# High and low halves for all six pieces of the experts' down projection

## The chip, the cores and the metric

The kernel runs on one core of a Trainium2 chip. The metric is the device time of one execution in microseconds. Lower is better. A core has five engines that run their own instruction streams and meet only at semaphores: PE (matmuls), DVE, ACT, POOL and SP, which here only issues the DMAs.

## The reference

A network of nine blocks on 256 tokens of 192 channels: four attention blocks and five mixture-of-experts blocks, each behind a layer norm and added to its input. The expert blocks that matter here (0, 1 and 3; 3 stands in the reference's "conv" place) compute, with W1 of 192x768 and W2 of 768x192 for each expert:

```
t = layer_norm(x)
gates = softmax or top-2 of (t @ Wg)          # 8 experts, some with a ninth that all tokens use
h = act(t @ W1[e] + b1[e])                    # relu, tanh-gelu, gelu
y = h @ W2[e] + b2[e]
x = x + sum over e of gates[:, e] * y
```

Every expert is computed for all tokens and its result is weighted by the gate. Block 2 gathers tokens instead, and block 4 has a gated form with a hidden size of 384.

## The kernel before

All of it is one program for one core, with the order of each engine written out by hand and a counting semaphore for each kind of result. Tokens are two tiles of 128. Blocks 0, 1 and 3 have 8, 8 and 9 experts, 25 in all. Experts 0 and 1 are written out, the middle ones run in a loop of two per turn, and the last ones are written out again.

The weights are float32. To use the faster fp32r matmul without losing precision the up projection is made from halves: `w1_hi` is a rounded copy made by ACT, `w1_lo` is the difference made by DVE (line 1193, three instructions of 128x512 per expert, called w_lo in the trace), and x has halves as well. The up projection of one expert is 30 matmuls of 256 columns (line 951) in three parts b = 0, 1, 2. After each part ACT makes two pieces of hid (line 600).

The down projection has six pieces of 128 hidden channels. Before, the first two (part b = 0) are plain float32 matmuls of 192 columns (line 963, each of which the trace shows as two records), and the last four use halves: DVE casts hid to `hid_hi` (line 1267) and subtracts to `hid_lo` (line 1269), POOL makes the high half of the down weights by a multiplication by one (line 443) and the low half by a subtraction (line 445). For each piece and token tile PE then does hid_hi times both halves of W2 (384 columns, line 975) and hid_lo times the high half (192 columns, line 977). The products with W2's low half are kept in their own 192 columns and DVE adds both column groups to x (lines 1282 and 1288, "the adds").

What sets the order around this:

- PE: up projection of expert g, then its down projection, then expert g+1. The down projection waits for the adds of the expert before, since both use the same two banks.
- ACT: hid of the three parts, then the three copies to `w1_hi` for the next expert. After expert 0 of a block it also makes the exponentials of the router's logits (`logit_exps`, line 582), from which DVE makes the gates (lines 1243 to 1250) before the first adds.
- DVE: halves of hid for two parts, three `w1_lo` of the next expert, the adds.
- POOL: halves of W2 of the next expert, each as soon as PE has released the part of `w2_hl` (`w2_used`, and `y_psum` for the last).
- The layer norm ahead of a block: DVE's statistics, the power on POOL (line 391), four DVE instructions that make xn (lines 1047 and 1050), PE's transposes (line 653), xT on ACT and DVE, the first up part, and the router's matmuls (line 928). POOL's program puts the split of expert 0's W2 right after the power. PE does some matmuls on a constant (line 661) while it waits.

## Time and profile before

| | us |
|---|---|
| median of 3 runs | 514.72 (511.82 to 517.03) |
| the profiled execution | 511.37 |
| its span, first to last instruction | 509.5 |
| PE busy in it | 463.6 |
| DVE busy | 354.0 |
| ACT busy | 234.8 |
| POOL busy | 171.3 |
| mean granted clock of PE | 0.98 |

The profile is that of one execution. The span is cut by blocks roughly as follows: block 0 from 57 to 127, block 1 from 174 to 244, block 3 from 371 to 447, block 4 from 450 to the end, with attention and block 2 between them. Busy is the time in which an engine executes an instruction, and that includes time in which an instruction that has started cannot go on. An idle time in brackets stands ahead of an instruction, with what ended it.

### The profile page before, as it was taken

The page shows a single profiled execution, that of the slowest core. Times are in us where ns is not written, and L with a number is a line of the kernel's source. Part 1 is how long each engine was busy: PE and PEld are TensorE (multiplying, and loading weights), DVE is VectorE, ACT ScalarE, POOL GpSimd, SP SyncE. Part 2 cuts the span into 40 slices and gives each one's busy share as a digit, 9 for nine tenths or more (in the row PEclk, how much of TensorE's full clock was granted, in tenths as well). Part 3 has the DMA queues.
Part 4 walks back from the last instruction along what each step waited for, and adds up shares of the span by engine and source line. Part 5 has one row for each costly group of instructions (what it writes and reads, how often), then busy time and mean ns, then how long its engine had stood idle before and what let it go on. Part 6 is the DMA issues. An engine that isn't in the chain of part 4 may idle for free.

```text
span 509.5 us, 8914 instructions
## 1 busy us (share of the span) xinstructions
PE 463.6 (91%) x3064; PEld 382.4 (75%) x3064; DVE 354.0 (69%) x780; ACT 234.8 (46%) x594; POOL 171.3 (34%) x171
## 2 busy tenths in 40 slices
PE   4989699999889799999889988899969999989997
PEld 3755499999555499999645654555759999979997
DVE  6575588998476578998476467451179899868764
ACT  1267245544156366555156337423218555627443
POOL 6026324673025415754006214310033665500000
PEclk8999999999999989999999999999989999989999
DMA  5380025650191015551169500602313555525551
GB/s 146 121 248 1 1 96 183 184 187 1 65 305 40 0 64 196 180 175 39 43 170 322 176 0 1 186 2 93 124 37 134 185 185 176 191 58 166 200 177 36
DMA packets 19347, 62.36 MB, mean 122 GB/s; under 512 B 4025, under 2 KB 6898, under 8 KB 19314
## 3 DMA queue, kind: packets, MB, share of 16 engines
q1 hardware_dynamic: 19314, 61.93, 38.0%
q8 instruction: 20, 0.33, 0.3%
q14 instruction: 13, 0.11, 0.1%
HBM read 59.82 MB, written 2.10 MB: 122 GB/s over the span
## 4 chain that ended last, share of the span: by engine, by line
PE 69%; DVE 11%; issue 10%; POOL 4%; DMA 3%; ACT 1%; SPq 1%; POOLq 0%; DVEq 0%
PE bank L951 24%; PE bank L963 10%; PE bank L975 7%; PE bank L766 6%; PE bank L805 3%; PE bank L977 3%; PE bank L792 3%; DVE xn L1047 3%; PE bank L661 2%; POOL rstd L391 1%; DMA rel<-rel_scratch 1%; PE bank L653 1%; PE bank L773 1%; DVE nmax L1153 1%; PE bank L674 1%
## 5 line engine op out<-in xcount | busy, mean ns | idle before, releaser
L951 PE MATMUL bank<-xT_hi,w_hi 128*128 128x256 f32 x408 | 111.7, 295 | 0.0
L600 ACT ACTIVATE hid<-bank,b 128x256 f32<-128x256 f32 x150 | 62.7, 471 | 71.0 <-PE bank L951 70.8
L1193 DVE TENSOR_TENSOR w_lo<-w,w_hi 128x512 fp32r<-128x512 f32 x102 | 93.0, 950 | 2.2 <-ACT w_hi L552 0.3
L951 PE MATMUL bank<-xT_hi,w_lo 128*128 128x256 f32 x408 | 82.6, 284 | 0.0
L443 POOL TENSOR_TENSOR w_hl<-w,consts 128x384 fp32r<-128x384 f32 x50 | 52.4, 1048 | 85.1 <-PE bank L977 85.1
L951 PEld LDWEIGHTS bank<-xT_hi,w_hi 128*128 128x128 f32 x408 | 79.2, 194 | 1.5 <-issue 1.1
L423 POOL TENSOR_TENSOR probs<-probs,rinv 128x512 f32<-128x512 f32 (+1 forms) x44 | 42.8, 991 | 101.0 <-DVE rinv L1157 100.9
L951 PEld LDWEIGHTS bank<-xT_hi,w_lo 128*128 128x128 f32 x408 | 64.3, 194 | 0.0
L975 PE MATMUL bank<-w_hl,hid_hi 128*128 128x384 f32 x200 | 61.7, 373 | 0.0
L445 POOL TENSOR_TENSOR w_hl<-w,w_hl 128x384 fp32r<-128x384 f32 x50 | 57.9, 1158 | 3.9
L963 PE MATMUL bank<-w,hid 128*128 128x192 f32 x308 | 56.5, 327 | 2.3 <-issue 2.3
L951 PE MATMUL bank<-xT_lo,w_hi 128*128 128x256 f32 x204 | 58.3, 286 | 0.0
L552 ACT ACTIVATE w_hi<-w 128x512 fp32r<-128x512 f32 x102 | 58.3, 626 | 0.1
L963 PEld LDWEIGHTS bank<-w,hid 128*128 128x128 f32 x308 | 49.5, 190 | 3.5 <-issue 2.9
L977 PE MATMUL bank<-w_hl,hid_lo 128*128 128x192 f32 x200 | 50.1, 251 | 0.0
L526 ACT ACTIVATE probs<-bank,nmax 128x256 f32<-128x256 f32 (+1 forms) x96 | 42.9, 461 | 10.3 <-DVE nmax L1153 10.3
L661 PE MATMUL bank<-warm 128*128 128x256 f32 x168 | 46.5, 419 | 1.2 <-DVE warm L1329 1.2
L766 PE MATMUL bank<-kT,qT 128*128 128x512 f32 (+1 forms) x96 | 42.6, 578 | 1.0 <-POOL probs L423 0.8
L951 PEld LDWEIGHTS bank<-xT_lo,w_hi 128*128 128x128 f32 x204 | 39.8, 195 | 0.2
L661 PEld LDWEIGHTS bank<-warm 128*128 128x128 f32 x168 | 33.7, 211 | 7.0 <-issue 1.9
L977 PEld LDWEIGHTS bank<-w_hl,hid_lo 128*128 128x128 f32 x200 | 38.1, 191 | 0.0
L975 PEld LDWEIGHTS bank<-w_hl,hid_hi 128*128 128x128 f32 x200 | 37.5, 188 | 0.7
(159 smaller groups left out, 674.3 us busy)
## 6 DMA issues: line engine op xcount, KB each, us to landing
w<-in_M_w_dram SPq DMA_DIRECT2D x34, 768.0 KB, 5.5
w<-in_M_w_dram SPq DMA_DIRECT2D x33, 576.0 KB, 3.9
w<-in_M_w_dram SPq DMA_DIRECT2D x9, 288.0 KB, 2.9
wqkv<-in_A_wqkv_dram SPq DMA_DIRECT2D x4, 432.0 KB, 7.0
rel_scratch<-relall SPq DMA_DIRECT2D x4, 372.0 KB, 2.3
wproj<-in_A_wproj_dram SPq DMA_DIRECT2D x4, 288.0 KB, 7.9
wqkv<-in_M_w_dram SPq DMA_DIRECT2D x2, 576.0 KB, 17.4
kT<-in_M_w_dram SPq DMA_DIRECT2D x2, 576.0 KB, 6.6
```

The lines of the kernel that those rows point to most:

```text
L443: pool.tensor_tensor(parts[:, :, 0], w, one, ALU.mult).then_inc(w2_hi_ready, 1)
L445: pool.tensor_tensor(parts[:, :, 1], w, parts[:, :, 0].bitcast(F32), ALU.subtract).then_inc(w2_lo_ready, 1)
L526: act.activation(probs[:, p % 2, t, h, 0:keys_of(n, t)], scores_bank(n, p, t)[:, h], ACT.Exp, bias=nmax[:, p % 2, t, h:h + 1], accum_out=r ...
L552: act.activation(w1_cols(w1_hi, b), w1_cols(w1[s], b), ACT.Copy).then_inc(w1_hi_ready, 1)
L600: ins = act.activation(hid[:, 2 * b + c, :], bank[B_H[b]][:, c * T:(c + 1) * T], FUNC[cfg["act"]], bias=b1[:, kb, bass.ds(at, 1)])
L661: pe.matmul(bank[b][:, 0:T], warm[:, 0:P], warm[:, :], start=True, stop=True)
L766: pe.matmul(scores_bank(n, p, t), qT[:, p, t * P:(t + 1) * P], kT[:, p, :, 0:keys_of(n, t)], start=True, stop=True).then_inc(s_psum, 1)
L951: ins = pe.matmul(bank[B_H[b]][:, c2 * T:(c2 + 1) * T], w, xs, start=(q == 0), stop=(q == 4))
L963: ins = pe.matmul(bank[B_Y[t]][:, 0:C], hid[:, c, t * P:(t + 1) * P], w2[s][:, c * C:(c + 1) * C], start=(c == 0), stop=(c == nc2 - 1), sk ...
L975: pe.matmul(out[:, 0:2 * C], hid_hi[:, c, tok], w2_hl[:, c].rearrange("p a n -> p (a n)"), start=False, stop=(c == SC - 1), skip_group_che ...
L977: ins = pe.matmul(out[:, 0:C], hid_lo[:, c, tok], w2_hl[:, c, 0], start=False, stop=(c == SC - 1), skip_group_check=True)
L1193: dve.tensor_tensor(w1_cols(w1_lo, b), w1_cols(w1[s], b), w1_cols(w1_hi, b).bitcast(F32), ALU.subtract)\
```

## The change

SB, the number of parts of the down projection with halves, becomes 3, so that no plain piece is left in blocks 0, 1 and 3.

- PE's down projection is 12 pairs of matmuls (384 and 192 columns) instead of 8 plain records and 8 pairs. Its first piece waits for `hid_lo` and `w2_lo` of part 0, where it waited for hid alone.
- `hid_hi` of part 0 is made by ACT, right after hid of part 0; DVE only subtracts for it. Parts 1 and 2 stay as they were.
- The high halves of W2 are made by ACT as copies (`split_down`), three of 128x384 per expert, behind the copies of w1, and with the same waits for PE that POOL had; POOL only subtracts, three times instead of twice. For expert 0 of a block they stand behind `x_transposed`, and for expert 1 ahead of `logit_exps`.
- `hid` has no memory of its own any more and lies in that of the attention's `probs`; a tile of block 2 moves from `hid` to `silu_g`.

```diff
-SB = 2
+SB = HB
@@
-        hid = sb("hid", [P, 2 * HB, T])
+        hid = probs[:, :, :, :, :].rearrange("p a t h k -> p (a t h) k")[:, 0:2 * HB, :]
@@
-        hplaceT = hid[:, 0:HB, :].rearrange("p c t -> p (c t)")
+        hplaceT = silu_g[:, :, :].rearrange("p c t -> p (c t)")
@@ POOL
-                pool.wait_ge(w2_in[s], 16 * (j + USED[m][s] + 1))
                 for b in range(SB):
-                    if not very_first:
-
-                        if b < SB - 1:
-                            pool.wait_ge(w2_used, g)
-                        else:
-                            pool.wait_ge(y_psum, 2 * g)
...
-                    pool.tensor_tensor(parts[:, :, 0], w, one, ALU.mult).then_inc(w2_hi_ready, 1)
                     pool.wait_ge(w2_hi_ready, SB * g + b + 1)
                     pool.tensor_tensor(parts[:, :, 1], w, parts[:, :, 0].bitcast(F32), ALU.subtract).then_inc(w2_lo_ready, 1)
@@ ACT
+            def split_down(m, j, i):
+
+                s = (i + SHIFT[m]) % 2
+                g = 2 * j + BASE[m] + i
+                very_first = isinstance(g, int) and g == 0
+                act.wait_ge(w2_in[s], 16 * (j + USED[m][s] + 1))
+                for b in range(SB):
+                    if not very_first:
+
+                        if b < SB - 1:
+                            act.wait_ge(w2_used, (SB - 1) * (g - 1) + b + 1)
+                        else:
+                            act.wait_ge(y_psum, 2 * g)
+                    at = 2 * b * C
+                    w = w2[s][:, at:at + 2 * C].rearrange("p (c n) -> p c n", c=2)
+                    act.activation(w2_hl[:, 2 * b:2 * (b + 1), 0], w, ACT.Copy).then_inc(w2_hi_ready, 1)
@@
+                        if cfg["split2"] and b == 0:
+                            act.wait_ge(h_ready, 3 * (2 * j + g) + 1)
+                            act.activation(hid_hi[:, 0:2, :], hid[:, 0:2, :], ACT.Copy).then_inc(hid_hi_act, 1)
...
                     for b in range(HB if cfg["split2"] and not last else 0):
                         split(m, j + i, 1 - i, b)
+                    if cfg["split2"] and not last:
+                        split_down(m, j + i, 1 - i)
...
+                if cfg["split2"]:
+                    split_down(m, 0, 0)
                 expert(0, 0)
                 logit_exps()
                 expert(0, 1)
@@ PE
-                                      start=False, stop=(c == SC - 1), skip_group_check=True)
+                                      start=(c == 0), stop=(c == SC - 1), skip_group_check=True)
...
-                        if c == 1:
+                        if c % 2 and c < SC - 1:
                             ins.then_inc(w2_used, 1)
@@ DVE
-                        if cfg["split2"] and b >= HB - SB:
...
+                        if cfg["split2"]:
+                            g = 2 * j + BASE[m] + i
+                            if b == 0:
+                                dve.wait_ge(hid_hi_act, g + 1)
+                            else:
+                                dve.wait_ge(h_ready, 3 * g + b + 1)
+                                dve.tensor_copy(hid_hi[:, 2 * b:2 * b + 2, :], hid[:, 2 * b:2 * b + 2, :]).then_inc(hid_hi_ready, 1)
+                                dve.wait_ge(hid_hi_ready, (SB - 1) * g + b)
+                            dve.tensor_tensor(hid_lo[:, 2 * b:2 * b + 2, :], hid[:, 2 * b:2 * b + 2, :],
+                                              hid_hi[:, 2 * b:2 * b + 2, :].bitcast(F32), ALU.subtract).then_inc(hid_lo_ready, 1)
```

## Rows read from the trace of the kernel before

**Rows 1.** The page's first part: busy us, share of the span, instructions.
```profile
PE 463.6 (91%) x3064; PEld 382.4 (75%) x3064; DVE 354.0 (69%) x780; ACT 234.8 (46%) x594; POOL 171.3 (34%) x171
```

**Rows 2.** Windows, one steady expert: start:end, us, busy us by engine, clock, DMA share, GB/s.
```profile
89.32:96.53 7.21, 7.21 (x57) 7.16 (x56) 6.84 (x12) 4.08 (x9) 4.52 (x5) 1.00 0.66 191
```

**Rows 3.** Chain that ended last, the plain down projection of a steady expert: start, us, what.
```profile
92.94 1.30 PE bank L963 x8
```

**Rows 4.** By source line, single instructions: duration ns min/median/max, first and last start.
```profile
L1193 DVE TENSOR_TENSOR w_lo<-w,w_hi x2: 1316/1410/1504, 95.6 to 96.9; 128x512 fp32r<-128x512 f32 x2
...
L445 POOL TENSOR_TENSOR w_hl<-w,w_hl x1: 1348/1348/1348, 96.5 to 96.5; 128x384 fp32r<-128x384 f32 x1
...
L445 POOL TENSOR_TENSOR w_hl<-w,w_hl x1: 1019/1019/1019, 99.1 to 99.1; 128x384 fp32r<-128x384 f32 x1
...
L1269 DVE TENSOR_TENSOR hid_lo<-hid,hid_hi x48: 691/692/694, 70.4 to 436.8; 128x512 fp32r<-128x512 f32 x48
```

**Rows 5.** Timeline of a steady expert of block 0: start, us, engine, line, instruction.
```profile
96.37 0.30 PE L951 MATMUL bank<-xT_hi,w_hi 128*128 128x256 f32 x1
...
97.90 0.84 ACT L600 ACTIVATE hid<-bank,b 128x256 f32<-128x256 f32 x2 [2.43 <-PE bank L951]
...
99.96 0.47 DVE L1267 CAST hid_hi<-hid 128x512 fp32r<-128x512 f32 x1 [0.29 <-ACT hid L600]
...
99.99 1.47 PE L963 MATMUL bank<-w,hid 128*128 128x192 f32 x8
...
100.46 0.69 DVE L1269 TENSOR_TENSOR hid_lo<-hid,hid_hi 128x512 fp32r<-128x512 f32 x1
```

**Rows 6.** Timeline of the layer norm ahead of block 0.
```profile
58.62 0.87 DVE L1047 TENSOR_SCALAR xn<-x,moments,rstd 128x192 f32<-128x192 f32 x1 [0.58 <-POOL rstd L391]
```

**Rows 7.** Timeline of the layer norm ahead of block 4.
```profile
450.85 0.38 DVE L1047 TENSOR_SCALAR xn<-x,moments,rstd 128x192 f32<-128x192 f32 x1 [0.58 <-POOL rstd L391]
```

**Rows 8.** Chain that ended last: router of block 0, gates' transposes, router of block 4.
```profile
66.50 0.64 PE bank L928 x5
...
81.91 0.22 PE bank L993 x2
...
455.90 0.64 PE bank L928 x5
```

**Rows 9.** Groups by line and shape, ACT: count | busy us, mean ns | idle before.
```profile
L552 ACT ACTIVATE w_hi<-w 128x512 fp32r<-128x512 f32 x102 | 58.3, 626 | 0.1
...
L582 ACT ACT_TABLE_LOAD x3 | 3.8, 1283 | 0.1
L564 ACT ACTIVATE hplace<-bank 128x384 f32<-128x384 f32 x8 | 3.6, 492 | 1.2 <-PE bank L859 1.2
```

**Rows 10.** Timeline of experts 0 and 1 of block 0.
```profile
69.17 0.37 DVE L1222 SCALAR_TENSOR_TENSOR sel<-consts,top_f,first 128x8 f32<-128x8 f32 x2
...
70.00 1.47 PE L963 MATMUL bank<-w,hid 128*128 128x192 f32 x8
...
73.55 0.30 PE L951 MATMUL bank<-xT_hi,w_hi 128*128 128x256 f32 x1
...
74.59 0.98 DVE L1243 TENSOR_TENSOR chosen<-expl,sel 128x16 f32<-128x16 f32 x1
...
77.24 0.73 DVE L1288 SCALAR_TENSOR_TENSOR x<-bank,gates,x 128x192 f32<-128x192 f32 x2
...
78.07 1.54 PE L963 MATMUL bank<-w,hid 128*128 128x192 f32 x8 [0.75 <-issue]
```

**Rows 11.** Timeline, PE: first transposes of the norms of block 0 and attention 1.
```profile
60.55 0.44 PE L653 MATMUL bank<-consts,xn 128*128 128x128 f32 x2 [2.36 <-DVE xn L1050]
...
129.81 0.71 PE L653 MATMUL bank<-consts,xn 128*96 128x128 f32 x4 [1.35 <-DVE xn L1047]
```

**Rows 12.** Windows with the granted clock (third figure from the end) in those two norms.
```profile
62.42:65.84 3.42, 3.42 (x12) 3.01 (x13) 2.64 (x7) 0.66 (x2) 0.00 (x0) 0.50 0.00 0
...
126.00:131.00 5.00, 3.61 (x19) 2.49 (x17) 3.54 (x13) 0.38 (x1) 0.69 (x1) 1.00 0.00 0
```

More of the change, by code:

```diff
@@ L219, in metaformer_kernel @@
         hid_hi_ready, hid_lo_ready = sem("hidden_high_ready"), sem("hidden_low_ready")
+        hid_hi_act = sem("hidden_high_first_ready")
         w2_hi_ready, w2_lo_ready, w2_used = sem("w2_high_ready"), sem("w2_low_ready"), sem("w2_parts_used")
@@ L429, in split @@
                 g = 2 * j + BASE[m] + i
-                very_first = isinstance(g, int) and g == 0
-                pool.wait_ge(w2_in[s], 16 * (j + USED[m][s] + 1))
                 for b in range(SB):
-                    if not very_first:
-                        if b < SB - 1:
-                            pool.wait_ge(w2_used, g)
-                        else:
-                            pool.wait_ge(y_psum, 2 * g)
-                    at = 2 * (HB - SB + b) * C
+                    at = 2 * b * C
                     w = w2[s][:, at:at + 2 * C].rearrange("p (c n) -> p c n", c=2)
                     parts = w2_hl[:, 2 * b:2 * (b + 1)]
-                    one = consts[:, CONST["ones"]][:, 0:1].unsqueeze(1).broadcast_to([P, 2, C])
-                    pool.tensor_tensor(parts[:, :, 0], w, one, ALU.mult).then_inc(w2_hi_ready, 1)
                     pool.wait_ge(w2_hi_ready, SB * g + b + 1)
@@ L552, in split @@
                 act.activation(w1_cols(w1_hi, b), w1_cols(w1[s], b), ACT.Copy).then_inc(w1_hi_ready, 1)
+            def split_down(m, j, i):
[9 more added lines that the diff above has]
+                            act.wait_ge(y_psum, 2 * g)
+                    at = 2 * b * C
+                    w = w2[s][:, at:at + 2 * C].rearrange("p (c n) -> p c n", c=2)
+                    act.activation(w2_hl[:, 2 * b:2 * (b + 1), 0], w, ACT.Copy).then_inc(w2_hi_ready, 1)
             def places():
@@ L1262, in hidden @@
                                 .then_inc(glu_ready, 1)
-                        if cfg["split2"] and b >= HB - SB:
-                            part = b - (HB - SB)
-                            sb2 = 2 * part
-                            dve.wait_ge(h_ready, 3 * (2 * j + BASE[m] + i) + b + 1)
-                            dve.tensor_copy(hid_hi[:, sb2:sb2 + 2, :], hid[:, 2 * b:2 * b + 2, :]).then_inc(hid_hi_ready, 1)
-                            dve.wait_ge(hid_hi_ready, SB * (2 * j + BASE[m] + i) + part + 1)
-                            dve.tensor_tensor(hid_lo[:, sb2:sb2 + 2, :], hid[:, 2 * b:2 * b + 2, :],
-                                              hid_hi[:, sb2:sb2 + 2, :].bitcast(F32), ALU.subtract).then_inc(hid_lo_ready, 1)
+                        if cfg["split2"]:
[8 more added lines that the diff above has]
+                                              hid_hi[:, 2 * b:2 * b + 2, :].bitcast(F32), ALU.subtract).then_inc(hid_lo_ready, 1)
                         if not cfg["split2"] and not last:
```

## The prediction

> **What bounds the kernel now.** I read, in this order, the page's busy times, one steady expert by windows, the chain that ended last, single experts in order of time, and the layer norms ahead of the expert blocks. PE is busy for 91% of the span [rows 1]. In the expert loops DVE is nearly full too: an expert takes 7.21 us, of which PE works 7.21, DVE 6.84, POOL 4.52 and ACT 4.08 [rows 2]. PE does 3.62 us of up projection (96.37 to 99.99) [rows 5], then 1.30 of plain down projection (8 matmul records) [rows 3], and the rest, 7.21 - 3.62 - 1.30 = 2.29, is split down projection (16 records). So PE sets the pace, and DVE has under 0.4 us to spare.
>
> DVE's 6.84 us hold a hidden part. A subtraction of 128x512 takes 0.69 us where POOL is idle (48 of hid's), but two of the three w_lo of an expert take 1.32 and 1.50 [rows 4]. These run while POOL splits the down weights, and POOL's subtraction takes 1.35 there and 1.02 alone [rows 4]. So they take turns: each waits until the other's whole instruction is done, and POOL costs DVE 0.63 + 0.81 = 1.44 us per expert.
>
> The same happens where nothing hides it. In the layer norms of blocks 0, 1 and 3 POOL splits the first expert's down weights while DVE makes xn: the first of the four xn instructions takes 0.87; in block 4, without the split, it takes 0.38 [rows 6, 7]. PE waits for them.
>
> The Trainium skill (SBUF — State Buffer, "Who interferes with whom") says that VectorE and GpSimd share a port pair that one of them holds for the whole instruction while "the other **fully blocks**". The trace agrees: 1.50 against 0.69 us.
>
> **The change, part by part.**
>
> *PE.* Per expert it takes away the 8 plain records (1.30) and adds 8 split ones. The pair of 384 and 192 columns costs 2.29/8 = 0.286, so down becomes 12 x 0.286 = 3.44 instead of 3.59: -0.15.
>
> *A new wait at the start of down.* The plain pieces needed only hid. Now the first piece needs hid's high half (ACT) and low half (DVE) of piece 0. Counted from the first up matmul, hid 0 starts on ACT at +1.53 (97.90) and takes 0.84: +2.37 [rows 5]. A wait for a result just made costs 0.04 (cast done 99.96 + 0.465, subtraction at 100.46): +2.41. The high half has the shape of an up weight's, 0.63 [rows 9]: +3.04. DVE follows with 0.04 + 0.69: +3.77. PE wakes 0.10 later (last add of expert 0 done at 77.97, first matmul 78.07) [rows 10]: +3.87. Without a stall down starts at +3.62. PE stands 0.25, plus up to 0.07 of restart (eight plain records take 1.54 there, 1.47 without a stall) [rows 5, 10]; I take 0.29. Period: 3.62 + 0.29 + 3.44 = 7.35 against 7.21, +0.14.
>
> *Does DVE follow in 7.35?* It gains a 0.61 (spacing of queued subtractions): 7.45, if POOL blocked it as before. But POOL's two high halves go to ACT, and its three subtractions start later. ACT ends the w1 copies at about +6.3; its first w2 copy, 128x384, is nearest to 0.49 (the same size from PSUM) and 0.63 (512 columns) [rows 9]; I take 0.55. POOL starts at +6.84, when two of DVE's three w_lo (from +6.0, after the later hid_lo 2) are done or running. Only the third is blocked (0.81); POOL's other two fall mostly under the adds, which take 0.73 per two beside POOL or not [rows 10]. DVE: 6.84 + 0.61 - 0.63 = 6.82, it fits. But POOL's last subtraction ends at about +3.15 of the next expert, and hid_lo 0 wants its inputs at +3.2: close (rival A). ACT, by the spacing of queued copies, about 0.1 under their length: 4.08 + 0.52 + 3 x 0.44 = 5.9 of 7.35, it fits; its third w2 copy waits for the end of down, more than 1 us before the next hid. POOL: 3 x 1.02 to 1.35, less than now.
>
> *Steady experts:* 8 + 8 + 9 less the first two of each block, 19. 19 x 0.14 = **+2.7**; bounds 19 x -0.15 = -2.9 (no stall) and 19 x 0.45 = +8.6 (DVE blocked again).
>
> *The layer norm.* POOL now has nothing to split until ACT has made a high half, which stands behind the transposed x. From the first xn to the router block 0 took 58.62 to 66.50, 7.88 us; blocks 1 and 3 show the same pattern, 7.60 and 7.87 (three such stretches, block 0's rows are shown). Block 4 needed 450.85 to 455.90, 5.05 [rows 6 to 8]. Gain 2.83 + 2.55 + 2.82 = **-8.2**. PE's granted clock was 0.50 (the 1.2 GHz level) for 3.42 us there, in block 4 too, after PE had stood 2.36 us in block 0; before attention 1 it stood 1.35 and the stretch shows 1.00 [rows 11, 12]. The idle shrinks by 1.3 to about 1.1, so the clock may stay at 2.4 GHz. It would save up to 0.09 on each of ten up matmuls, less what other engines set: -0.6 per block.
>
> *First expert's down.* Its hid_lo 0 stands on DVE behind the router's selection, done at 69.54, while down starts at 70.00 [rows 10]; 0.69 + 0.10 later is a stall of 0.35. With the higher clock PE comes earlier but DVE does not, since POOL blocks its two w_lo: 0.8. Less 0.15 for the pairs: +0.6 or +2.0 over three blocks. With the norm: -8.2 + 0.6 = -7.6, or -10.0 + 2.0 = -8.0; I take **-7.8**.
>
> *Second expert.* ACT's exponentials for the gates stood behind three w1 copies; now they stand behind the third w2 copy too, which waits for the end of down 0. They end about +1.2 into up 1, +2.5 in blocks 1 and 3 with a table load of 1.28 [rows 9]. DVE's three w_lo end at about +2.0 and its first gate instruction waits for POOL's third subtraction, to +2.9. It waited in block 0 too (0.98 us, ending 75.57, +2.02) [rows 10]. From there to the last add took 2.4. So down starts at 2.9 + 2.4 + 0.65 (hid_lo 0) + 0.1 = +6.05 where it was +4.52 (78.07 less 73.55), and then takes 3.51 where it was 3.84 (to 81.91) [rows 8]: +1.2 per block, **+3.6**; bounds 0 (if something else hides it) and +2.3 per block.
>
> Sum: 2.7 - 7.8 + 3.6 = -1.5 us. The profiled execution took 511.37 us (span 509.5) and becomes 509.9. The median of the runs is 514.72, 0.65% above that execution: 513.2.
>
> **Rivals.**
>
> *A: the turns with POOL decide (ends slower).* If POOL's last subtraction still runs when DVE wants hid_lo 0, that takes up to 0.88 more, all of it before PE's down. For: my margin is under 0.1 us. Against: a stall of PE does not delay ACT's copies, so the longer it is, the earlier POOL is done in the next expert; it damps itself. Price: period 7.66, +8.6 instead of +2.7: 519.1. It decides from a POOL end later than +3.2.
>
> *B: no stall.* If the high half and the subtraction take 0.25 less together, the period is 7.06, -2.9 instead of +2.7, and the first stall goes too (-0.9): 506.7. Against: both durations come from 48 or 102 rows that hardly vary.
>
> *C: the clock falls in a worse place.* 3.42 us at half clock cost 1.7 us of PE work. In block 4 over half of it lay on transposes and warming matmuls. If it lay on the up projection, each block gave back 1.0: 516.2. Against: less idle than before a stretch that stayed at 1.00.
>
> *D: the gate chain costs more.* Exponentials between two table loads, then hid 0 of expert 1: 1.2 more in blocks 1 and 3, 515.6. For: ACT's chain ends close behind DVE's. Against: DVE is the later of the two.
>
> **How the numbers follow.** Main forecast 0.45, 510.5 to 516 (at 513.2); A 0.18; B 0.13; C 0.12; D 0.12. 1% (5.1 us) is about what a measurement of this kernel tells from no change: under 509.6 is faster, over 519.9 slower. Faster: B's 0.13 and 0.11 of the main case, where the runs' own spread (511.82 to 517.03) or a larger clock gain carry it over. Slower: 0.10 of A, 0.06 of C and D together or with A. Same: 0.60. Range: B's 506.7 to A's 519.1, rounded outward: 506.5 to 519.5.
>
> **What would show it.** Right: xn takes 0.3 to 0.4 us in blocks 0, 1 and 3; POOL has no high halves and 75 subtractions; 300 split matmuls of each kind; steady experts of 7.3 to 7.4 us with an idle of 0.2 to 0.3 between up and down; expert 1 near 9.6 instead of 8.4; a lower mean of w_lo. Wrong: steady experts under 7.2 (B) or over 7.5 with hid_lo above 0.75 us (A); the low clock over up matmuls (C); hid 0 of expert 1 later than +4 (D). The forecast fails most easily in the steady experts, where 0.1 us each is 1.9 us.

## The result and the profile after

| | before | changed |
|---|---|---|
| median, same chip | 512.68 us | 518.42 us |
| profiled execution, span | 509.5 | 516.2 |
| PE / DVE / ACT / POOL busy | 463.6 / 354.0 / 234.8 / 171.3 | 465.9 / 357.7 / 282.7 / 156.1 |

The ratio of changed to before is 1.0084, interval [1.0052, 1.0115]: slower by 0.84%, 4.3 us. The ratio counts only executions within 1.5% of their kernel's fastest, so it is not the quotient of the two medians. The forecast of 513.2 against the median of 514.72 was a ratio of 0.997. The change was run once more on another chip, with the last experiments: 1.0051 [1.0009, 1.0093].

The page of the changed kernel, first the engines (busy us, share, instructions), then groups (count | busy us, mean ns | idle before and what ended it):

```profile
PE 465.9 (90%) x3064; PEld 381.2 (74%) x3064; DVE 357.7 (69%) x805; ACT 282.7 (55%) x694; POOL 156.1 (30%) x146
...
L436 POOL TENSOR_TENSOR w_hl<-w,w_hl 128x384 fp32r<-128x384 f32 x75 | 94.0, 1277 | 108.0 <-ACT w_hl L560 107.8
...
L990 PE MATMUL bank<-w_hl,hid_hi 128*128 128x384 f32 x300 | 94.2, 380 | 13.3 <-DVE hid_lo L1286 11.7
L1208 DVE TENSOR_TENSOR w_lo<-w,w_hi 128x512 fp32r<-128x512 f32 x102 | 90.3, 924 | 2.1
```

The parts changed as the diff says: 300 split matmuls, 75 subtractions on POOL and no multiplication there, 48 us more on ACT [rows 1]. New is the idle time of 13.3 us ahead of line 990, the first split matmul, of which 11.7 us end with `hid_lo`.

To see where the time went, I cut both executions at the same events. "Norm" runs from the first xn instruction of a block to its first up matmul, "expert 0" from there to the first up matmul of expert 1, and so on; "rest" ends with the last add of the block.

| us | before | changed | difference, three blocks |
|---|---|---|---|
| norm, blocks 0 / 1 / 3 | 5.62 / 5.63 / 5.38 | 2.88 / 2.88 / 2.88 | -7.98 |
| expert 0 | 9.31 / 9.02 / 9.54 | 9.91 / 9.84 / 9.90 | +1.78 |
| expert 1 | 8.33 / 8.33 / 8.28 | 11.05 / 11.52 / 11.51 | +9.15 |
| rest | 45.55 / 45.62 / 53.03 | 46.73 / 46.87 / 54.13 | +3.51 |
| block 4 (norm and expert 0) | 3.13 + 7.96 | 2.88 + 7.46 | -0.75 |
| all else | | | +1.0 |
| span | 509.5 | 516.2 | +6.7 |

"All else" is code that both kernels share, and it is not steady: up to the first xn the profiled executions of this study take 56.8 to 60.0 us, and between blocks 1 and 3 from 127.8 to 134.2. So of the 6.7 us between the two spans only the 4.3 us of the ratio can be claimed for the change. The parts inside the blocks are steadier: a norm takes 2.88 in each of the three blocks here. Block 4 is not: it is the same code in both kernels, and it is shorter here because no half clock fell there (more on this below).

**The layer norm** did what was forecast. Timeline of the changed kernel, DVE, block 0 (start, us, ..., idle before in brackets):

```profile
59.98 0.38 DVE L1062 TENSOR_SCALAR xn<-x,moments,rstd 128x192 f32<-128x192 f32 x1 [0.58 <-POOL rstd L392]
```

0.38 where it was 0.87 [rows 6], and the clock in these norms is 1.00 in all three blocks, where 3.4 us of each were at 0.50 ([rows 12] has block 0's).

**The steady expert** nearly did: 7.36 to 7.48 us inside the loops, where the kernel before takes 7.20 to 7.28. Windows of the changed kernel (us, busy us of PE, PEld, DVE, ACT, POOL, clock, DMA share, GB/s), one steady expert:

```profile
98.60:106.00 7.40, 7.31 (x56) 7.13 (x55) 6.81 (x13) 5.95 (x13) 3.73 (x4) 1.00 0.57 186
```

and its start in the timeline:

```profile
98.05 3.68 POOL L436 TENSOR_TENSOR w_hl<-w,w_hl 128x384 fp32r<-128x384 f32 x3 [3.67 <-ACT w_hl L560]
...
98.61 0.30 PE L966 MATMUL bank<-xT_hi,w_hi 128*128 128x256 f32 x1
...
100.14 0.84 ACT L608 ACTIVATE probs<-bank,b 128x256 f32<-128x256 f32 x2 [0.80 <-PE bank L966]
...
101.00 0.63 ACT L613 ACTIVATE hid_hi<-probs 128x512 fp32r<-128x512 f32 x1
...
101.67 0.69 DVE L1286 TENSOR_TENSOR hid_lo<-probs,hid_hi 128x512 fp32r<-128x512 f32 x1 [0.49 <-ACT hid_hi L613]
...
102.47 0.41 PE L990 MATMUL bank<-w_hl,hid_hi 128*128 128x384 f32 x1
```

(`probs` is hid here, since it lies in that memory now.) Each link of the new wait is there: hid 0 at +1.53, high half at +2.39, low half at +3.06, PE at +3.86. POOL's last subtraction ends at 101.73, +3.12.

**The second expert** did not. Timeline of block 0 in the changed kernel, first DVE and ACT, then PE:

```profile
74.49 0.98 DVE L1258 TENSOR_TENSOR chosen<-expl,sel 128x16 f32<-128x16 f32 x1
...
77.03 0.73 DVE L1305 SCALAR_TENSOR_TENSOR x<-bank,gates,x 128x192 f32<-128x192 f32 x2
...
77.69 0.68 DVE L1286 TENSOR_TENSOR hid_lo<-probs,hid_hi 128x512 fp32r<-128x512 f32 x1
...
78.63 0.41 PE L990 MATMUL bank<-w_hl,hid_hi 128*128 128x384 f32 x1 [2.08 <-DVE hid_lo L1286]
```

PE stands for 2.08 us and starts at +5.85 of an expert whose up projection began at 72.78. Then the clock falls. Windows of the changed kernel, the three stretches at clock 0.50 that lie in the blocks:

```profile
79.30:82.71 3.41, 3.41 (x15) 3.41 (x14) 3.38 (x6) 0.61 (x2) 1.41 (x1) 0.50 0.05 16
...
198.77:202.18 3.41, 3.41 (x15) 3.41 (x14) 3.38 (x5) 2.01 (x5) 1.56 (x2) 0.50 0.00 0
396.74:400.15 3.41, 3.39 (x13) 3.41 (x14) 3.34 (x7) 2.57 (x6) 0.28 (x1) 0.50 0.10 35
```

All three lie over the second expert's down projection. There 15 matmuls pass in 3.41 us, and a pair of 384 and 192 columns takes 0.53 us instead of 0.29. The expert takes 11.05 to 11.52 us. The kernel before had four such stretches in the blocks: at 62.42, 178.48 and 376.45 from the norm into the first expert, and one in block 4.

In blocks 1 and 3 PE stands longer than in block 0. Timeline of block 1 in the changed kernel, ACT and PE:

```profile
194.03 1.28 ACT L608 ACT_TABLE_LOAD   x1
...
197.81 0.41 PE L990 MATMUL bank<-w_hl,hid_hi 128*128 128x384 f32 x1 [2.55 <-DVE hid_lo L1286]
```

The table load (the reload of ACT's function table between the exponentials and the block's own activation) stands ahead of hid 0 there. Block 0 has none.

### The profile page after: what moved, and what is told of

The parts are those of the page before. It is cut to its first block, busy times and chain, and to the rows that moved or that the text cites. A ratio compares the mean times of both kernels' runs of the same rounds, so it can differ in the third digit from the quotient of the medians.

```text
span 516.2 us, 9046 instructions
## 1 busy us (share of the span) xinstructions
PE 465.9 (90%) x3064; PEld 381.2 (74%) x3064; DVE 357.7 (69%) x805; ACT 282.7 (55%) x694; POOL 156.1 (30%) x146
## 4 chain that ended last, share of the span: by engine, by line
PE 62%; DVE 10%; issue 4%; ACT 4%; POOL 2%; DMA 1%; SPq 0%; POOLq 0%; ACTq 0%; DVEq 0%
PE bank L966 19%; PE bank L990 12%; PE bank L992 5%; PE bank L781 4%; PE bank L978 3%; PE bank L820 3%; PE bank L807 2%; PE bank L874 2%; PE bank L926 2%; PE bank L788 1%; DVE nmax L1168 1%; POOL rstd L392 1%; DVE w_lo L1208 1%; PE bank L715 1%; PE bank L764 1%
## 5 line engine op out<-in xcount | busy, mean ns | idle before, releaser
L436 POOL TENSOR_TENSOR w_hl<-w,w_hl 128x384 fp32r<-128x384 f32 x75 | 94.0, 1277 | 108.0 <-ACT w_hl L560 107.8
L990 PE MATMUL bank<-w_hl,hid_hi 128*128 128x384 f32 x300 | 94.2, 380 | 13.3 <-DVE hid_lo L1286 11.7
L992 PE MATMUL bank<-w_hl,hid_lo 128*128 128x192 f32 x300 | 77.2, 257 | 0.0
L608 ACT ACTIVATE probs<-bank,b 128x256 f32<-128x256 f32 x150 | 62.3, 468 | 25.0 <-PE bank L966 23.3
L990 PEld LDWEIGHTS bank<-w_hl,hid_hi 128*128 128x128 f32 x300 | 58.9, 196 | 17.9 <-issue 17.7
L1286 DVE TENSOR_TENSOR hid_lo<-probs,hid_hi 128x512 fp32r<-128x512 f32 x75 | 51.9, 692 | 17.6 <-ACT hid_hi L613 15.8
L992 PEld LDWEIGHTS bank<-w_hl,hid_lo 128*128 128x128 f32 x300 | 60.0, 200 | 0.0
L560 ACT ACTIVATE w_hl<-w 128x384 fp32r<-128x384 f32 x75 | 36.8, 521 | 20.6 <-PE bank L992 20.6
L676 PE MATMUL bank<-warm 128*128 128x256 f32 x168 | 43.0, 395 | 1.2 <-DVE warm L1346 1.2
L1168 DVE TENSOR_REDUCE nmax<-bank 128x2 f32<-128x512 f32 (+1 forms) x48 | 30.5, 651 | 4.7 <-PE bank L781 4.3
```

The costliest lines, as they stand in the source:

```text
L436: pool.tensor_tensor(parts[:, :, 1], w, parts[:, :, 0].bitcast(F32), ALU.subtract).then_inc(w2_lo_ready, 1)
L608: ins = act.activation(hid[:, 2 * b + c, :], bank[B_H[b]][:, c * T:(c + 1) * T], FUNC[cfg["act"]], bias=b1[:, kb, bass.ds(at, 1)])
L676: pe.matmul(bank[b][:, 0:T], warm[:, 0:P], warm[:, :], start=True, stop=True)
L990: pe.matmul(out[:, 0:2 * C], hid_hi[:, c, tok], w2_hl[:, c].rearrange("p a n -> p (a n)"), start=(c == 0), stop=(c == SC - 1), skip_group_ ...
L992: ins = pe.matmul(out[:, 0:C], hid_lo[:, c, tok], w2_hl[:, c, 0], start=False, stop=(c == SC - 1), skip_group_check=True)
L1286: dve.tensor_tensor(hid_lo[:, 2 * b:2 * b + 2, :], hid[:, 2 * b:2 * b + 2, :], hid_hi[:, 2 * b:2 * b + 2, :].bitcast(F32), ALU.subtract).t ...
```

## The experiments

The theory after this: the forecast is right on the layer norms and nearly right on the steady experts, and what it lacks is the half clock over the second expert's down projection, plus a little in the first experts. The rivals: that the loss is in the order of ACT's exponentials; that the six pieces cost it by their own work; or that the move of the copies to ACT costs it. The first five edits below are made to the changed kernel, the next three to the kernel before. Four of these five were executed only once, so their whole times prove little; what counts of them is the trace.

### The exponentials ahead of the copies

```diff
                     for b in range(HB if cfg["split2"] and not last else 0):
                         split(m, j + i, 1 - i, b)
+                    if isinstance(j, int) and j == 0 and i == 0:
+                        logit_exps()
                     if cfg["split2"] and not last:
                         split_down(m, j + i, 1 - i)
@@
                 expert(0, 0)
-                logit_exps()
                 expert(0, 1)
```

> The changed kernel, but ACT makes the exponentials of the router's logits before the copies of the second expert's down weights, as the kernel before did. In the changed kernel the second expert takes 11.05, 11.52 and 11.51 us (first up matmul to first up matmul), before 8.33, 8.33 and 8.28. Theory 1 (DVE's turns with POOL set the gates): block 0 hardly changes (10.8 to 11.1), blocks 1 and 3 lose some 0.3 to 0.5 us each, and the clock still falls in all three. Theory 2 (ACT's third copy, which waits for the end of the first down projection, sets them): each of the three loses 1.5 us or more, and where PE stands under 1.5 us the clock stays up, which gives another 1.7 us.

Measured: 517.33 us (one execution), span 515.4; second experts 11.10, 9.02 and 9.02. In block 0 nothing moved, for DVE's turns with POOL come last there, and the half clock fell there again (75.96 to 79.37). In blocks 1 and 3 the down projection starts earlier. PE stood 2.55 us there in the changed kernel and stands 1.64 now:

```profile
193.75 0.41 PE L991 MATMUL bank<-w_hl,hid_hi 128*128 128x384 f32 x1 [1.64 <-DVE hid_lo L1287]
```

The window of that whole expert shows clock 1.00:

```profile
188.34:197.35 9.01, 7.37 (x58) 7.17 (x57) 8.75 (x17) 7.54 (x15) 4.59 (x5) 1.00 0.43 153
```

So of the 2.5 us 0.9 is the shorter wait, and the other 1.6 is the clock. Neither theory held as it was put: blocks 1 and 3 gained more than the first allows, and block 0 gained nothing, against the second. The exponentials matter in the two blocks whose activation has a table of its own, and are not the whole loss. The total did not fall as far as the blocks did, since between blocks 1 and 3 this execution took 134.2 us instead of 127.8, with a stretch of half clock of its own (297.83 to 308.07).

### PE kept at work ahead of the second down projection

```diff
                     pe.wait_ge(w2_in[s], 16 * (j + USED[m][s] + 1))
+                    if cfg["split2"] and isinstance(j, int) and j == 0 and i == 1:
+                        stay_warm(4, 7)
                     pe.wait_ge(acc_done, 2 * (2 * j + g))
```

> The changed kernel, but PE makes four matmuls on the constant (8 records of about 0.22 us, 1.7 us in all) into a free bank while it waits to start the down projection of expert 1, in blocks 0, 1 and 3. They take no time from the wait, which is 2.2 to 2.7 us long. Theory (the half clock over down 1 comes from PE's standing there): no half clock in the second experts; each goes from 11.05, 11.52, 11.51 to about 9.4, 9.9, 9.9 us, some 4.9 us in all. Rival (the clock falls for another reason, or the extra time of down 1 is not the clock's): the second experts stay within 0.3 us of theirs.

Measured: 512.95 us (one execution), span 511.1; second experts 9.43, 9.82 and 9.81. Timeline of PE in block 0, then the window over the down projection:

```profile
75.67 1.89 PE L676 MATMUL bank<-warm 128*128 128x256 f32 x8
77.81 0.41 PE L992 MATMUL bank<-w_hl,hid_hi 128*128 128x384 f32 x1 [0.26 <-issue]
```

```profile
78.50:81.90 3.40, 3.40 (x27) 3.37 (x26) 3.37 (x6) 1.40 (x3) 2.01 (x2) 1.00 0.05 17
```

The down projection starts nearly where it did, at +5.75 (changed kernel +5.85; in blocks 1 and 3 +6.17 and +6.32). The gap ahead of it is filled, and in the same 3.4 us 27 matmuls pass instead of 15. That is 1.6 to 1.7 us per block, of which the earlier start is 0.1 to 0.15: the half clock is a cost by itself, and in this execution it did not come when PE was kept at work there. By itself this execution could be chance, since the stretch can fail to come without any edit (below, the changed kernel once more). With the two repairs together, six filled gaps of six stayed at 1.00.

### The products of the high halves first

```diff
-                    for c in range(nc2 - plain):
+                    for c in range(2 if cfg["split2"] else 0):
+                        if c == 0:
+                            pe.wait_ge(hid_hi_act, 2 * j + g + 1)
+                            pe.wait_ge(w2_lo_ready, SB * (2 * j + g) + 1)
...
+                    for c in range(2 if cfg["split2"] else 0):
+                        if c == 0:
+                            pe.wait_ge(hid_lo_ready, SB * (2 * j + g) + 1)
...
+                    for c in range(2, nc2 - plain):
```

The lines left out are the same matmuls of part 0 in another order: those with hid_hi for both pieces and both token tiles, then those with hid_lo.

> The changed kernel, but PE takes part 0 of every down projection in another order: the four matmuls with hid's high half first, which need only ACT's copy, and then the four with the low half. Theory (in steady experts PE stands 0.25 us for hid_lo of part 0, and nothing else): the period goes from 7.38 to 7.06 to 7.15 us, and the time falls by 19 x 0.27 = 5 us, to about 0.998 of the kernel before. Rival (DVE or its turns with POOL are the bound by now): the period stays at 7.3 or more and PE stands at another place, at the up projection for w_lo or at a later part.

Measured: 513.56 us, ratio 1.0037 [0.9993, 1.008]; steady experts 7.35 to 7.48 (the first in block 0 8.12), second experts 9.41, 9.76 and 9.71. The first half of the expectation held: down starts on time (+3.6). The period stays. Timeline of the steady expert that begins at 97.28:

```profile
101.08 0.43 DVE L1301 CAST hid_hi<-probs 128x512 fp32r<-128x512 f32 x1
101.54 0.69 DVE L1303 TENSOR_TENSOR hid_lo<-probs,hid_hi 128x512 fp32r<-128x512 f32 x1
...
102.28 0.19 PEld L1007 LDWEIGHTS bank<-w_hl,hid_hi 128*128 128x128 f32 x1 [0.27 <-DVE hid_lo L1303]
```

The wait of 0.26 moved from part 0 to part 1. ACT's extra copy (0.63) stands ahead of hid 1, so cast and subtraction of part 1 are late as well. The first wait hid a second one of the same size; to take one away brings nothing. So the rival of the expectation held, and the theory of 7.06 to 7.15 us did not. In the second experts the gap is split in two (1.23 and 0.33 us in block 1), and no half clock follows.

### POOL makes the high halves again, six pieces

```diff
+                    one = consts[:, CONST["ones"]][:, 0:1].unsqueeze(1).broadcast_to([P, 2, C])
+                    pool.tensor_tensor(parts[:, :, 0], w, one, ALU.mult).then_inc(w2_hi_ready, 1)
                     pool.wait_ge(w2_hi_ready, SB * g + b + 1)
@@
-                    if cfg["split2"] and not last:
-                        split_down(m, j + i, 1 - i)
```

(with the waits of `split_down` moved to POOL as well.)

> The changed kernel, but POOL makes the high halves of the down weights again (three multiplications and three subtractions per expert, with the waits that ACT's copies had), so only hid's high half is on ACT. Theory (the move to ACT is what freed the norms and what spares DVE in the loop): the norms take 5.4 to 5.6 us again from the first xn to the first up matmul, POOL's six instructions per expert block DVE three to five times, and a steady expert goes from 7.38 to 7.6 to 8.2 us. Rival (DVE has room, and the chain through ACT's hid copy alone sets the period): steady experts stay within 0.05 us of 7.38, and only the norms change.

Measured: 561.56 us (one execution; the kernel before has a median of 516.5 on this chip), span 559.7. The norms take 5.63 again. Steady experts take 7.4 to 11.1 us, where 7.6 to 8.2 were expected, with stretches of half clock among them. Timeline of DVE in one that takes 8.55, and its window:

```profile
103.51 2.73 DVE L1214 TENSOR_TENSOR w_lo<-w,w_hi 128x512 fp32r<-128x512 f32 x2
...
107.47 1.09 DVE L1292 TENSOR_TENSOR hid_lo<-probs,hid_hi 128x512 fp32r<-128x512 f32 x1
...
110.61 3.97 DVE L1214 TENSOR_TENSOR w_lo<-w,w_hi 128x512 fp32r<-128x512 f32 x3
```

```profile
103.64:112.19 8.55, 7.63 (x54) 7.27 (x55) 8.48 (x13) 4.60 (x10) 6.21 (x6) 1.00 0.48 161
```

DVE is busy for 8.48 of 8.55 us: with six instructions on POOL all three w_lo and the first `hid_lo` (1.09 instead of 0.69) wait for turns. This is rival A of the forecast as it looks when it decides. The six pieces need the move of the copies to ACT; without it they are 8.7% slower than the kernel before on the same chip, with it 0.84%. A part of that is half clock (mean 0.951 here).

### DVE makes the high half of part 0

```diff
-                        if cfg["split2"] and b == 0:
-                            act.wait_ge(h_ready, 3 * (2 * j + g) + 1)
-                            act.activation(hid_hi[:, 0:2, :], hid[:, 0:2, :], ACT.Copy).then_inc(hid_hi_act, 1)
@@
                             if b == 0:
+                                dve.wait_ge(h_ready, 3 * g + 1)
+                                dve.tensor_copy(hid_hi[:, 0:2, :], hid[:, 0:2, :]).then_inc(hid_hi_act, 1)
                                 dve.wait_ge(hid_hi_act, g + 1)
```

> The changed kernel, but DVE casts hid's high half of part 0 as it does for parts 1 and 2, and ACT's copy for it goes away. Theory (two chains stand close together: the one through ACT's copy, and DVE's own sum, 6.84 + 0.61 - 0.63 us and now 0.4 to 0.5 more): hid_lo 0 would be ready 0.2 earlier, but DVE now needs 7.3 us and more and meets POOL's third subtraction, so a steady expert takes 7.4 to 8.0 us. Rival (only ACT's copy makes the wait): the stall at the start of down is gone and the period falls to 7.1 to 7.25.

Measured: 530.15 us (one execution), span 528.3; steady experts 7.3 to 8.05.

```profile
100.55 0.92 DVE L1279 CAST hid_hi<-probs 128x512 fp32r<-128x512 f32 x1
101.50 0.69 DVE L1285 TENSOR_TENSOR hid_lo<-probs,hid_hi 128x512 fp32r<-128x512 f32 x1
```

```profile
98.14:105.76 7.62, 7.23 (x56) 7.06 (x55) 7.52 (x14) 5.52 (x12) 3.87 (x4) 1.00 0.52 181
```

The cast that takes 0.42 alone takes 0.92 here, beside POOL's subtraction, and DVE is busy for 7.52 of 7.62. So the copy on ACT, which looks like a mere 0.63 in the chain, keeps DVE from becoming the bound.

### The kernel before, POOL's split of expert 0 held back

```diff
                     if MOE[n]["split2"]:
+                        pool.wait_ge(w1_lo_ready, 3 * BASE[n] + 3)
                         for i in range(2):
```

> The kernel before with one wait more: POOL starts to split expert 0's down weights only when DVE has made all three w_lo of expert 0, so behind the layer norm. Nothing else is changed. Theory (a third of the story of the changed kernel is that its norms lost POOL): from the first xn to the first up matmul 2.9 us in place of 5.62, 5.63 and 5.38, -8 us, and the clock stays up there, which takes about 0.9 more from each first expert: 499 to 502 us of span, 0.980 of the kernel before. Rival (the gain of the norm is given back in the first or second expert, as in the changed kernel): under 4 us in all.

Measured: 505.72 us, ratio 0.9876 [0.983, 0.9923], where 0.980 was expected. The norms take 2.88 in all three blocks, so the gain in the norms does not need the change at all. But expert 0 takes 9.7 instead of 9.0 to 9.5. DVE's short instructions of the router's selection now run beside POOL:

```profile
65.11 0.71 DVE L1213 TENSOR_SCALAR nmax_l<-top 128x2 f32<-128x2 f32 x1
...
66.63 1.18 DVE L1220 TENSOR_SCALAR first<-consts,top_f 128x8 f32<-128x8 f32 x2
```

In the kernel before the same two take 0.17 and 0.36. A part of the gain is given back this way, and the same happens in the first expert of the changed kernel.

### The kernel before, only the copies moved to ACT

```diff
-                    pool.tensor_tensor(parts[:, :, 0], w, one, ALU.mult).then_inc(w2_hi_ready, 1)
                     pool.wait_ge(w2_hi_ready, SB * g + b + 1)
@@
+            def split_down(m, j, i):
+
...
+                    act.activation(w2_hl[:, 2 * b:2 * (b + 1), 0], w, ACT.Copy).then_inc(w2_hi_ready, 1)
```

(`split_down` and its calls as in the change, for the four pieces.)

> The kernel before (two plain and four split pieces) with one part of the change alone: ACT makes the high halves of the down weights, two copies per expert, in the places where the change puts them, and POOL only subtracts. Theory (the change's gain in the norms and its loss in the second experts both come from this part, the loss of the steady experts from the six pieces): norms -2.7, -2.7, -2.5 us; steady experts 7.20 to 7.22 as before; second experts 10.5 to 11.5 us with a stretch of half clock in each; in all within 2 us of the kernel before. Rival (the second experts' loss belongs to the six pieces, whose hid_lo 0 stands behind the gates and adds on DVE): second experts at 8.3 to 9.3 us without half clock, and 5 to 8 us faster than before.

Measured: 503.97 us, ratio 0.9755 [0.9688, 0.9823]. Norms 2.88, expert 0 8.64 to 8.65, second experts 8.41, 9.16 and 9.16. A steady expert, by windows:

```profile
93.86:101.08 7.22, 7.22 (x57) 7.18 (x55) 6.18 (x12) 5.05 (x11) 2.62 (x3) 1.00 0.61 191
```

PE still sets 7.22 us; DVE fell from 6.84 [rows 2] to 6.18. The theory on record expected 10.5 to 11.5 us and half clock in the second experts and no gain in all; its rival held. PE stands 1.36 us ahead of the second down projection in blocks 1 and 3, and the clock is 1.00 there. So "the move to ACT costs it" is wrong: this half of the change gains 1.8 to 3.1% by the interval of four executions. The other half, the six pieces, is what loses. Between the two profiles it costs 3.7 us in the three first experts, 7.4 in the second ones and 3.5 in the rest, 14.6 us or 2.9%; by the ratios, from different chips, 3.4% (1.0084 / 0.9755).

### The kernel before, expert 0's split ahead of the norm

```diff
+                    if MOE[n]["split2"]:
+                        split(n, 0, 0)
                     ln(nln)
@@
-                        for i in range(2):
-                            split(n, 0, i)
+                        split(n, 0, 1)
```

> The kernel before with POOL's program in another order: it splits expert 0's down weights ahead of the power of the layer norm, where it idled 6.6 us and more, and not behind it. Nothing else is changed. With the split behind the norm (e4) the norms gained 8.0 us, but the first experts lost 1.3 because POOL then ran beside DVE's selection. Theory (what hurts is only that POOL works in a stretch where DVE's work is on the path): norms 2.9 us, first experts 8.3 to 8.6 in place of 9.31, 9.02, 9.54, second experts 8.2 to 8.4: 10 to 11 us less, 0.978 to 0.982 of the kernel before. Rival (something else bounds the first expert, or the split delays the end of attention): first experts at 9.5 or more, or a longer way to the first xn: no better than e4, 0.985 to 0.99.

Measured: 501.49 us, ratio 0.9734 [0.9686, 0.9783]. This is the lowest ratio, and it has not one instruction more than the kernel before: POOL idles ahead of the norm and makes expert 0's halves then, so that neither xn nor the router's selection runs beside it. Norms 2.88, expert 0 8.47, second experts 8.28. It differs from the one before it by less than the intervals.

Its profiled execution has one long stretch of half clock, from just ahead of the first up matmul of block 4 (444.30):

```profile
443.63:453.87 10.24, 9.98 (x43) 9.50 (x42) 6.36 (x23) 4.17 (x8) 0.00 (x0) 0.50 0.23 77
```

The first expert of block 4 takes 10.91 there, where it takes 7.46 in the changed kernel: what half clock costs depends on the work that it lies over, and it lies in other places than the waits named here too.

### The two repairs together, on the six pieces

The edits of the first two experiments in one kernel, with three warming matmuls (six records) instead of four (eight).

> The changed kernel with two repairs together: the second expert's exponentials stand ahead of the high-half copies, and three matmuls into a free bank run on the tensor engine before the second expert's down projection. Theory (what the change lost beyond its six pieces is the half clock over the second experts' down projections, and a little of a late table load in blocks 1 and 3): no stretch of clock 0.50 over those down projections, second expert 9.4, 9.0 and 9.0 us where the changed kernel had 11.05, 11.52 and 11.51, so 6 to 7 us less than the changed kernel; the steady period stays at 7.36 to 7.40; against the kernel before 0.995 to 1.001. Rival (the loss is in the six pieces' extra work itself, and the half clock only moves): the second experts stay at 11, or half-clock stretches stand in other places inside the blocks, and the ratio stays at 1.004 to 1.010.

Measured: 513.76 us, ratio 1.001 [0.9973, 1.0048]. The second experts take 9.36, 8.80 and 8.85 (expected 9.4, 9.0, 9.0), all at clock 1.00:

```profile
72.40:81.75 9.35, 8.67 (x64) 8.16 (x63) 9.09 (x18) 6.17 (x13) 4.27 (x4) 1.00 0.46 149
188.61:197.41 8.80, 8.68 (x64) 8.17 (x63) 8.54 (x17) 7.55 (x15) 4.53 (x5) 1.00 0.44 156
387.62:396.47 8.85, 8.67 (x64) 8.17 (x63) 8.59 (x17) 7.55 (x15) 4.58 (x5) 1.00 0.45 158
```

In the second experts the expected 6 to 7 us are gained against the first profiled execution of the changed kernel (7.1), but only 3.95 against its other one (next). In the medians of the executions that the ratios count it is 2.3 us on the same chip (513.76 against 516.06), and the intervals of the two ratios overlap, so a gain of the whole is not shown. The theory holds for the place and overstates the size: in other executions a second expert of the changed kernel escapes the half clock, and the half clock shows up elsewhere (here 262.95 to 266.36, in attention 2, and 454.10 to 457.51, in block 4). The mean granted clock over all compared executions is 0.989 for this kernel and 0.987 for the changed one, hardly different. A part of what the rival said is true.

### The changed kernel once more

> The changed kernel once more, nothing edited, on the same chip as the two others. Theory (the half clock follows the wait of 2.2 to 2.7 us before the second experts' down projection, so it is not an accident of one profiled execution): stretches of clock 0.50 over those down projections again, second expert 11.0 to 11.6 us in each of the three blocks, steady period 7.36 to 7.40, ratio 1.005 to 1.012. Rival (the stretches fell there by chance): they stand elsewhere, the second experts take 9.4 to 9.9 us, and the ratio is 0.995 to 1.005.

Measured: 518.09 us (516.06 in the six of ten executions that the ratio counts), ratio 1.0051 [1.0009, 1.0093]; second experts 9.51, 11.52 and 9.93. One of three expected stretches came, in block 1; blocks 0 and 3 escaped although PE stood as long. Timeline of PE at the first matmul of the second down projection in blocks 0, 1 and 3, and the window of the one stretch:

```profile
77.63 0.41 PE L990 MATMUL bank<-w_hl,hid_hi 128*128 128x384 f32 x1 [2.14 <-DVE hid_lo L1286]
```

```profile
195.02 0.41 PE L990 MATMUL bank<-w_hl,hid_hi 128*128 128x384 f32 x1 [2.56 <-DVE hid_lo L1286]
```

```profile
395.19 0.41 PE L990 MATMUL bank<-w_hl,hid_hi 128*128 128x384 f32 x1 [2.56 <-DVE hid_lo L1286]
```

```profile
196.25:199.66 3.41, 3.41 (x15) 3.41 (x14) 3.34 (x5) 1.73 (x4) 2.08 (x2) 0.50 0.00 0
```

This is the cleanest price of the half clock: the same code in the same block with the same wait takes 11.51 with it and 9.93 without (block 3), 11.05 and 9.51 (block 0), so 1.5 to 1.6 us. And it shows that the half clock need not follow the wait.

### Copies on ACT with the exponentials first, four pieces

The first experiment's edit, made to the kernel with only the copies moved.

> The kernel before with the down weights' high halves on the scalar engine (as in e8_before_act_high) and, new, the second expert's exponentials ahead of those copies. Theory (in blocks 1 and 3 the copies push the second table load behind the exponentials late, and the second expert's first hidden piece with it): second expert 8.3 us in blocks 1 and 3 instead of 9.16, 8.3 to 8.4 in block 0, some 1.7 us less than e8_before_act_high, ratio to the kernel before 0.970 to 0.977. Rival (the order of exponentials and copies is covered by the sums that follow): second expert 9.16 again and the ratio that of e8_before_act_high, 0.9755, within 0.002.

Measured: 503.72 us, ratio 0.9838 [0.976, 0.9916], where 0.970 to 0.977 was expected; second experts 8.38, 8.53 and 8.53. The profile shows the step (9.16 to 8.53 in blocks 1 and 3, less than the 8.3 expected):

```profile
184.79:193.32 8.53, 7.54 (x59) 7.34 (x57) 8.01 (x18) 7.15 (x16) 2.40 (x3) 1.00 0.46 163
```

The medians can't show 1.3 us: 503.72 here, 503.97 without the edit, and the two ratios, from different chips, overlap. Whether it is worth anything in total stays open.

Another comparison is within one chip: the six pieces with both repairs took 513.76 us and this kernel, with four pieces, 503.72. So even without the half clock over the second experts the six pieces cost about 2%. Between the two profiles 3.7 us of it are in the first experts, 1.6 in the second and 3.4 in the rest.

## Why the prediction was wrong

It forecast 0.3% less (1.5 us by its sum), and 0.84% more came (4.3 us). By its own terms, against the profiled executions:

| term | forecast | measured |
|---|---|---|
| steady experts, 19 | +2.7 | +3.5 |
| norm and first expert | -7.8 | -6.2 |
| second expert | +3.6 | +9.2 |
| block 4 and shared code | 0 | +0.3 |

**The step that failed is the second expert.** The forecast put the start of its down projection at +6.05 and the down projection at 3.51 us. The start was nearly right: +5.85 in block 0 and +6.32 in blocks 1 and 3, where the second table load stands ahead of hid 0 (rival D had 1.2 us for it; the start moved by 0.5 against block 0). The down projection took 5.2 us. Without the half clock the same expert took 9.51 in block 0 and 9.93 in block 3, where the sum gives 9.56. So the term the forecast put at nothing is 1.5 to 1.6 us of half clock per second expert: three of three in one profiled execution, one of three in the other.

The forecast knew both sides of it. It had seen in [rows 11, 12] that the clock is 0.50 after PE has stood 2.36 us, it had priced such a stretch (1.7 us of PE work), and it had lengthened PE's wait ahead of the second down projection from 0.75 [rows 10] to over 2 us in its own sum. It did not put the two together: it asked whether the half clock would leave the norm, and in rival C whether it would fall on the up projection, but not whether the wait it had just made was as long as the one that it had taken away.

**The first expert was undersized.** Norm and first expert together gained 6.2 and not 7.8. The norm did even a little more than forecast: from the first xn to the router's first matmul 4.14 us in each block, where the kernel before took 7.72, 7.44 and 7.71, so -10.4 beside the -10.0 that the forecast had with the clock up. The loss is behind it. The down projection did not get shorter by 0.15, it takes 3.54 (69.24 to 72.78) after 3.55 (70.00 to 73.55), and it starts late, at 69.24, +6.37. Timeline of DVE and PE there:

```profile
63.25 2.82 DVE L1208 TENSOR_TENSOR w_lo<-w,w_hi 128x512 fp32r<-128x512 f32 x2
...
66.46 0.51 DVE L1227 TENSOR_SCALAR nmax_l<-top 128x2 f32<-128x2 f32 x1
...
68.29 0.69 DVE L1286 TENSOR_TENSOR hid_lo<-probs,hid_hi 128x512 fp32r<-128x512 f32 x1
```

```profile
69.24 0.41 PE L990 MATMUL bank<-w_hl,hid_hi 128*128 128x384 f32 x1 [1.30 <-DVE hid_lo L1286]
```

The forecast had a stall of 0.8 there and it is 1.30: POOL's subtractions, which the change moves behind the norm, meet DVE's two w_lo (2.82 us for two) and then a short instruction of the selection (0.51 instead of 0.17).

**The steady expert was nearly right**: 7.36 to 7.48 against 7.35, start of down +3.86 against +3.87, the down projection 3.54 (102.47 to 106.01) against 3.44, DVE 6.81 against 6.82, POOL's end +3.12 against +3.15. Rival A therefore did not decide, and rival B's missing stall was there. The rest is 0.18 instead of 0.14 per expert, 0.8 us in all.

**What it had right about the clock** is that it stays up in the norms. PE stands 1.10 us there now (1.41 in block 3) and the clock was 1.00 in all three. In block 4 it was 1.00 as well, which the forecast had left alone (0.75 us gained), but that is luck: PE stood 1.94 us there, and after the same 1.94 us the half clock came in block 4 in the first, the third and the repaired variant of the changed kernel.

**The sum after the fact.** Forecast -1.5; norms and first experts +1.6; steady +0.8; second experts without half clock +0.9 (9.51, 9.93 and 9.93 take 4.5 more than before, forecast 3.6); half clock over the second experts 1.6 for each that falls. That is +3.4 with one of them, +5.0 with two and +6.6 with three, beside 4.3 by the ratio (and 6.7, with shared code, between two profiles, of which the changed one has three). The ratio fits one or two: the mean clock of 0.987 over the compared executions stands for some 13 us at half clock (an estimate: twice the missing share of the span), where the profiled execution, at 0.980, had 20.6. With both causes in the second expert taken away the six pieces stand at 1.001 [0.9973, 1.0048], beside a forecast of 0.997.

**What stays open.** Why some waits are followed by half clock and others are not. In the profiled executions of the changed kernel and of the one with the exponentials first, PE stood 2.08 to 2.56 us seven times ahead of a second down projection, and five were followed by it. In the two variants with POOL or DVE making high halves it stood 2.48 to 2.67 us six times there, and four were followed: nine of thirteen. Where it stood 1.64 us or less there, or was kept at work, none of eleven was. That is no safe length: the wait of 1.76 us ahead of attention 3, which all thirteen profiled executions have, was followed by half clock in three. And the kernel before has more half clock on the whole (mean 0.977 over the compared executions) than the changed one (0.987) and is still faster: in its norms the stretch lies partly over transposes and warming matmuls, which other engines hold back anyway. The place decides what it costs, and no run here measured it with its place alone changed.

## What to carry to other kernels

Each wait of PE that a forecast lengthens must be held against the waits in the same trace after which the granted clock fell; if it is as long, add the half clock over what follows, with a chance, or fill the gap. A change of two parts should be costed, and if possible timed, as two: here one part gained about 2.4% and the other gave back more, and the gain of the first was to be had by moving expert 0's split to where its engine idles. Where two engines take turns, look at what runs beside the moved instruction in every place it can land, the short instructions too.

## What the runs showed of the hardware

- Half clock over a dense down projection costs 1.5 to 1.6 us for a stretch of 3.41 us (11.51 against 9.93 and 11.05 against 9.51 in the same code). Eight warming matmul records, 1.89 us of work on a free bank, went with a clock of 1.00 in all three blocks, and six records did as well, in one profiled execution each. Without them the stretch came in four of six.
- Short DVE instructions suffer from the turns most, in proportion: a tensor_scalar of 128x2 takes 0.17 alone and 0.51 to 0.71 beside POOL's subtraction, and a cast of 128x512 0.42 alone and 0.92.
- A copy of 128x384 to fp32r takes ACT 0.52 us, and of 128x512 0.63. POOL's multiplication by one took 0.83 alone and its subtraction 1.02.
